# Two expert stages: each half of the tokens sorted once, slots ordered by levels of tiles, waits by level

## The chip, the core and the metric

The kernel runs on one core of one Trainium2 chip. The metric is device time in microseconds, from the first to the last instruction of one launch; smaller is better. All data is fp32 or the 32-bit type that TensorE reads as fp32r.

## The reference

An image batch (8, 128, 32, 32) goes through convolutional attention and whitening, is turned into 8192 tokens of 128 channels (64 tiles of 128 tokens), and passes two attention layers, each followed by a mixture of experts with 8 experts of which every token uses two:

```
probs = softmax(logits); top_p, top_idx = top_k(probs, 2)      # layer 2: gelu, hidden 512
t = t + sum_k w_k * (gelu(LN(t) @ W1[e_k] + b1[e_k]) @ W2[e_k] + b2[e_k])
h = silu(x @ w1[e].T) * (x @ w3[e].T); y = h @ w2[e].T         # layer 3: silu, hidden 341
t = t + sum_k gate_k * y[e_k]
```

Between the two lies window attention over 32 tokens. What is computed is the same before and after the change.

## The kernel before

**Sorting.** Each expert stage routes its tokens in two parts of 32 tiles (`PT`). `Route.place_in_pieces` works on VectorE (DVE): it finds the two best experts, counts tokens by expert, and works out `places`, the row to which each token's copy goes. Rows are slots of 256 rows (`UNIT`), and a slot belongs to one expert, whose number stands in `owners`. A list of `Plan` groups says which tiles are sorted together: `GELU_PLAN` sorts 12, 20 and 32 tiles, `SILU_PLAN` 32, 20 and 12. A group of n tiles takes (2·n·128 + 8·255)//256 slots, so 19, 27 and 39, in all 85 in each stage.

**Sending.** `send_tiles` runs on GpSimd (POOL): two indirect DMAs per tile (one for each chosen expert) write normalised rows into the DRAM scratch `sorted_rows`, with three in flight (`FLIGHT`).

**Units.** `Units` runs the slots as a software pipeline of NU + 4 steps on TensorE (PE). In step s it multiplies slot s-2 up, transposes slot s and multiplies slot s-4 down; its end frees the steps of ScalarE (ACT) and DVE of the same number. SyncE (SP) loads the slot's rows four ahead (`load(u)` waits for the end of step u-4) and stores results (`store(u)`); both stand in one queue. A load that is the first of its group also waits until all DMAs of the group's tiles have landed. In each step DVE drains the down product, makes the low half of x, copies the expert's weights, in silu gates the hidden values, adds results of earlier tiles that are due (`adds`, start step and group) and then runs one piece of the placing of part 1. That placing begins at step 0, and its sends follow on POOL.

**Fetching.** `Units.bring` on POOL waits until a group's slots are stored, and then issues two indirect DMAs per tile that read `sorted_results` into `fetch` buffers of 4 tiles (8 DMAs). There are two such buffers, so the fetch of one waits until the tiles fetched two buffers earlier are added. `add_result` adds two rows per token on DVE.

**Order of the work.** Queues are in program order, and a `Block` ends when all engines are through. The gelu stage has a routing block (part 0 placed; 16 sends; PE then computes biases behind `placed`), and a block with the units and the first half's window attention, which adds the remaining tiles four per step and in which POOL, behind its last fetch, makes the low halves of the silu weights (L2420). The silu stage has a block with the second window attention and the routing (part 0 is placed in its first step), then the silu units; at their end the last tiles are fetched and added and the tokens stored to `out`.

## Time and profile before

| what | value |
|---|---|
| median of 3 runs | 1424.36 us (1424.33 to 1430.51) |
| the profiled execution: time, span | 1423.12 us, 1421.4 us |
| PE busy | 1188.9 us, 84% |
| DVE busy | 919.4 us, 65% |
| POOL busy (issue of indirect DMAs above all) | 582.9 us, 41% |
| ACT busy | 560.4 us, 39% |
| indirect DMAs: sends, fetches | 256, 256 |

Some 1.7 us lie around the span. The clock that TensorE is granted is 1.00 of full through most of the gelu and silu units and 0.50 in the routing. In a timeline row "x9" means that nine instructions were merged; the row's second number is then the time from the first's start to the last's end. An idle time stands in brackets with what ended it.

### The profile page before, as it was taken

The page shows a single profiled execution, that of the slowest core. Times are in us where ns is not written, and L with a number is a line of the kernel's source. Part 1 is how long each engine was busy: PE and PEld are TensorE (multiplying, and loading weights), DVE is VectorE, ACT ScalarE, POOL GpSimd, SP SyncE. Part 2 cuts the span into 40 slices and gives each one's busy share as a digit, 9 for nine tenths or more (in the row PEclk, how much of TensorE's full clock was granted, in tenths as well). Part 3 has the DMA queues.
Part 4 walks back from the last instruction along what each step waited for, and adds up shares of the span by engine and source line. Part 5 has one row for each costly group of instructions (what it writes and reads, how often), then busy time and mean ns, then how long its engine had stood idle before and what let it go on. Part 6 is the DMA issues. An engine that isn't in the chain of part 4 may idle for free. (4 is left out here: it accounts for less than half of the span.)

```text
span 1421.4 us, 31172 instructions
## 1 busy us (share of the span) xinstructions
PE 1188.9 (84%) x11614; PEld 1028.8 (72%) x11614; DVE 919.4 (65%) x2231; ACT 560.4 (39%) x1293; POOL 582.9 (41%) x639
## 2 busy tenths in 40 slices
PE   7999998888574999999996673858589999999960
PEld 4555556668564999999994453636489999999960
DVE  4777775579671754466652876575539777788862
ACT  3444442245461655555554531543323333232310
POOL 3000002000136777774504772067300774566675
PEclk9999999899655999999997885779569999999985
DMA  8300000000502333343424210011012333333343
GB/s 311 129 0 1 0 1 9 1 0 1 142 14 69 115 130 123 123 124 103 115 65 165 53 46 2 1 45 54 28 37 66 116 120 99 103 111 115 108 131 107
DMA packets 85495, 109.63 MB, mean 77 GB/s; under 512 B 18179, under 2 KB 70950, under 8 KB 85094
## 3 DMA queue, kind: packets, MB, share of 16 engines
q1 hardware_dynamic: 65990, 62.92, 14.2%
q0 software_dynamic: 19360, 44.73, 9.9%
q8 instruction: 97, 1.59, 0.5%
q14 instruction: 48, 0.39, 0.1%
HBM read 53.19 MB, written 54.39 MB: 76 GB/s over the span
## 5 line engine op out<-in xcount | busy, mean ns | idle before, releaser
L1425 POOL DMA_INDIRECT sorted_rows<-s_normed,s_places x128 | 135.1, 1055 | 174.9 <-DVE s_places L1366 135.0
L1502 POOL DMA_INDIRECT gx_fetch<-sorted_results,g_places x128 | 131.9, 1030 | 121.8 <-DMA sorted_results<-gx_yq 53.4
L1502 POOL DMA_INDIRECT sx_fetch<-sorted_results,s_places x128 | 136.0, 1062 | 85.5 <-issue 33.1
L1585 PE MATMUL g_bank<-weights,gx_hT 128*128 x1360 | 165.8, 275 | 0.2 <-ACT gx_hT L1613 0.2
L1425 POOL DMA_INDIRECT sorted_rows<-g_normed,g_places x128 | 132.4, 1035 | 64.8 <-issue 35.4
L1585 PEld LDWEIGHTS g_bank<-weights,gx_hT 128*128 128x128 f32 x1360 | 158.5, 192 | 0.6 <-issue 0.6
L1548 PE MATMUL s_bank<-sx_xT_high,sx_w_now 128*128 128x256 f32 (+1 forms) x510 | 151.7, 298 | 1.2 <-DVE sx_hT L1660 0.6
L1550 PE MATMUL s_bank<-sx_xT_high,sx_w_now 128*128 128x256 f32 (+1 forms) x510 | 144.2, 283 | 0.0
L1549 PE MATMUL s_bank<-sx_xT_low,sx_w_now 128*128 128x256 f32 (+1 forms) x510 | 144.0, 282 | 0.0
L1613 ACT ACTIVATE gx_hT<-g_bank,gx_b_now 128x256 f32<-128x256 f32 x340 | 132.8, 481 | 3.1 <-PE g_bank L1585 3.0
L1585 PE MATMUL s_bank<-weights,sx_hT 128*128 (+1 forms) x1020 | 129.7, 276 | 2.9 <-DVE sx_yq L1671 1.4
L1585 PEld LDWEIGHTS s_bank<-weights,sx_hT 128*128 128x128 f32 (+1 forms) x1020 | 120.4, 191 | 6.4 <-issue 6.2
L1606 ACT ACTIVATE sx_xT_high<-s_bank 128x256 fp32r<-128x256 f32 x85 | 32.7, 385 | 225.5 <-PE s_bank L1585 210.1
L237 PE MATMUL attended<-probs,vs 128*128 128x512 f32 x256 | 120.3, 593 | 0.0
L339 ACT ACTIVATE probs<-score,nmax 128x1024 f32<-128x1024 f32 x64 | 71.3, 1115 | 113.1 <-DVE nmax L281 113.1
L281 DVE TENSOR_REDUCE nmax<-score 128x1 f32<-128x1024 f32 x64 | 78.2, 1223 | 45.6 <-PE score L226 45.6
L1548 PE MATMUL g_bank<-gx_xT_high,gx_w_now 128*128 128x256 f32 x340 | 104.0, 306 | 3.1 <-DVE gx_w_now L1643 2.0
L1669 DVE TENSOR_TENSOR gx_yq<-g_bank,weights 128x256 f32<-128x256 f32 x85 | 36.1, 425 | 99.8 <-PE g_bank L1585 97.5
L1550 PE MATMUL g_bank<-gx_xT_high,gx_w_now 128*128 128x256 f32 x340 | 96.9, 285 | 0.0
L1549 PE MATMUL g_bank<-gx_xT_low,gx_w_now 128*128 128x256 f32 x340 | 96.9, 285 | 0.0
L1606 ACT ACTIVATE gx_xT_high<-g_bank 128x256 fp32r<-128x256 f32 x85 | 32.7, 385 | 155.1 <-PE g_bank L1585 127.6
L1548 PEld LDWEIGHTS s_bank<-sx_xT_high,sx_w_now 128*128 128x128 f32 (+1 forms) x510 | 91.3, 179 | 1.7 <-issue 1.7
(423 smaller groups left out, 2718.2 us busy)
## 6 DMA issues: line engine op xcount, KB each, us to landing
gx_xq<-sorted_rows SPq DMA_DIRECT2D x85, 128.0 KB, 2.1
sorted_results<-gx_yq SPq DMA_DIRECT2D x85, 128.0 KB, 2.0
sx_xq<-sorted_rows SPq DMA_DIRECT2D x85, 128.0 KB, 2.1
sorted_results<-sx_yq SPq DMA_DIRECT2D x85, 128.0 KB, 2.0
sorted_rows<-zeros POOLq DMA_DIRECT2D x19, 512.0 KB, 11.2
feats<-in_x SPq DMA_DIRECT2D x8, 512.0 KB, 8.0
out<-tokens SPq DMA_DIRECT2D x16, 256.0 KB, 3.9
s_raw<-in_silu_up SPq DMA_DIRECT2D x1, 2736.0 KB, 10.0
```

The lines of the kernel that those rows point to most:

```text
L237: done = pe.matmul(out[:, HALF * h:HALF * h + HALF], vs[s % 4][:, :], probs[s % 4][:, HALF * h:HALF * h + HALF], start=(n == 0), stop=(n = ...
L281: dve.tensor_reduce(nmax[s % 4][:, :], score[s % 2][:, :], AX.X, ALU.max, negate=True).then_inc(max_ready, 1)
L339: act.activation(probs[s % 4][:, :], score[s % 2][:, :], ACT.Exp, bias=nmax[s % 4][:, 0:1], accum_out=zsum[s % 4][:, 0:1]).then_inc(exp_do ...
L1425: pool.indirect_dma_start(out=sorted_rows[g], out_offset=bass.IndirectOffsetOnAxis(ap=places[:, at, r:r + 1], axis=0), in_=normed[:, at, : ...
L1502: pool.indirect_dma_start(out=fetch[n % 2][:, i, r, :], out_offset=None, in_=self.sorted_results[g], in_offset=bass.IndirectOffsetOnAxis(a ...
L1548: pe.matmul(out, left[:, part, columns], right[0][:, :], start=True, stop=False)
L1549: pe.matmul(out, left[:, part, columns], right[1][:, :], start=False, stop=False)
L1550: pe.matmul(out, left[:, part + 1, columns], right[0][:, :], start=False, stop=True)
L1585: done = pe.matmul(down[u % 2][:, P * k:P * k + C], hT[u % 2][0:width, i, P * k:P * k + P], self.w_down[0:width, bass.ds(e, 1), i, :].rear ...
L1606: act.activation(xT[u % 2][0][:, :], self.turned[u % 2][:, 0:UNIT], ACT.Copy).then_inc(self.x_high, 1)
L1613: done = act.activation(hT[i][:, k, :], up[i][k // 2][:, k % 2, :], ACT.Gelu, bias=self.b_now[u % 4][:, k:k + 1])
L1669: dve.tensor_tensor(self.yq[u % 4][:, :, :], product, bias, ALU.add).then_inc(self.y_ready, 1)
```

## The change

Each part is one group: both plans have two groups of 32 tiles, 39 slots each, 78 in all. Within a group the slots are ordered by levels. A level is a number of tiles n with a kind: FULL levels end, for each expert, at the last slot that the first n tiles fill whole; BEGUN levels end at the last slot that they have begun. A load then waits for the tiles of its level (`tiles_needed`), and the fetch of the first n tiles waits for the slots up to a BEGUN level (`ready_tiles`). By the plan's arithmetic, gelu loads wait for 12 tiles at slot 0, 16 at slot 5, 24 at slot 9, 32 at slot 17, 48 at slot 39, all 64 at slot 48; silu loads for 32 at slot 0, 44 at slot 39 and 64 at slot 44. The gelu fetches wait for 39 slots (tiles to 32), 62 (to 48), 70 (to 56) and 78; the silu fetches for 23 (to 16), 39 (to 32), 58 (to 44), 66 (to 52), 74 (to 60) and 78. The placing has more instructions, since it shifts rows by level and finds owners by level. The silu fetches get four buffers, which lie in the `normed` tiles of part 0. The gelu adds begin at step 50 (before: 46 and 60), the silu adds at steps 45 and 73 (before: 49 and 77). Of scratch filled with zeros there are 94 slots of 128 KB in place of 85.

```diff
-GELU_PLAN = Plan([12, 20, 32], [(0, 2), (2, 3)])
-SILU_PLAN = Plan([32, 20, 12], [(0, 1), (1, 3)])
+FULL, BEGUN = False, True
+GELU_PLAN = Plan([[(12, FULL), (16, FULL), (24, FULL), (PT, BEGUN)],
+                  [(16, FULL), (16, BEGUN), (24, BEGUN), (PT, BEGUN)]])
+SILU_PLAN = Plan([[(16, BEGUN), (PT, BEGUN)],
+                  [(12, FULL), (12, BEGUN), (20, BEGUN), (28, BEGUN), (PT, BEGUN)]])
...
+    def units_of(self, tiles):
+        return (2 * tiles * P + E * (UNIT - 1)) // UNIT
+    def full_units_of(self, tiles):
+        return max(0, -(-(2 * tiles * P - E * (UNIT - 1)) // UNIT))
+    def tiles_needed(self, u):
+        g = self.group_of[u]
+        for n, begun in self.levels[g]:
+            if not begun and u - self.first_unit[g] < self.full_units_of(n):
+                return self.first_tile[g] + n
+        return self.first_tile[g + 1]
...
@@ place_in_pieces
-        for i, g in enumerate(groups):
-            steps.did(dve.tensor_tensor(of_group(before, i), of_group(before, i),
-                                        shift[:, i, :].unsqueeze(1).to_broadcast([P, plan.tiles[g], E]), ALU.add))
+        steps.did(dve.tensor_tensor(by_expert(count), by_expert(before), at_level(change, 0), ALU.add))
+        for i in range(1, L):
+            steps.then(dve.tensor_tensor(by_expert(passing), by_expert(before), at_level(from_row, i - 1), ALU.is_ge))
+            steps.then(dve.tensor_tensor(by_expert(passing), by_expert(passing), at_level(change, i), ALU.mult))
+            steps.then(dve.tensor_tensor(count[:, :], count[:, :], passing[:, :], ALU.add))
+            if i % 2 == 0:
+                yield
...
@@ Units.bring
+            for first, end, units in plan.ready_tiles(g):
+                for i in range(4):
+                    pool.wait_ge(self.y_stored[i], 16 * len(range(i, units, 4)))
+                for n in range(first // SEND, end // SEND):
+                    if n >= len(fetch):
+                        pool.wait_ge(self.added_both, (n + 1 - len(fetch)) * SEND)
...
@@ Units.sync, load(u)
-            if u == plan.first_unit[g]:
-                self.sent.wait_landed(sp, 2 * plan.first_tile[g + 1])
+            if u == 0 or plan.tiles_needed(u) > plan.tiles_needed(u - 1):
+                self.sent.wait_landed(sp, 2 * plan.tiles_needed(u))
...
-                          owners, group_rows, group_results, "gx_", banks, ((46, 0), (60, 1)), Tools(nc, brief))
+                          owners, group_rows, group_results, "gx_", banks, ((50, 0),), fetch, Tools(nc, brief))
...
-                      group_rows, group_results, "sx_", banks, ((49, 0), (77, 1)))
+                      group_rows, group_results, "sx_", banks, ((45, 0), (73, 1)), fetch)
```

Three places in the order of the engines follow. The first is DVE in the gelu routing block, where part 0 is placed: `g_room` holds all work arrays, the last rows end the slot numbers from which `g_places` is cut. (Semaphores are shown under the name that first used their number.) Before:

```order
L1343 TENSOR_TENSOR g_room<-g_room 128x12x8 [waits vs_ready]
L1343 TENSOR_TENSOR g_room<-g_room 128x20x8
L1351 TENSOR_TENSOR g_room<-g_room 128x96 [waits gr_exp_done,vs_ready]
L1351 TENSOR_TENSOR g_room<-g_room 128x160
L1354 TENSOR_REDUCE gr_slot_no<-g_room 128x32 [waits vs_ready]
L1351 TENSOR_TENSOR g_room<-g_room 128x96 [waits vs_ready]
L1351 TENSOR_TENSOR g_room<-g_room 128x160
L1354 TENSOR_REDUCE gr_slot_no<-g_room 128x32 [waits vs_ready]
```

The same place of the change:

```order
L1389 TENSOR_TENSOR g_room<-g_room,gr_change 128x256 [waits vs_ready]
L1391 TENSOR_TENSOR g_room<-g_room,gr_from_row 128x256
L1392 TENSOR_TENSOR g_room<-g_room,gr_change 128x256 [waits vs_ready]
L1393 TENSOR_TENSOR g_room<-g_room 128x256 [waits vs_ready]
L1391 TENSOR_TENSOR g_room<-g_room,gr_from_row 128x256 [waits vs_ready]
L1392 TENSOR_TENSOR g_room<-g_room,gr_change 128x256 [waits vs_ready]
L1393 TENSOR_TENSOR g_room<-g_room 128x256 [waits vs_ready]
L1391 TENSOR_TENSOR g_room<-g_room,gr_from_row 128x256 [waits vs_ready]
L1392 TENSOR_TENSOR g_room<-g_room,gr_change 128x256 [waits vs_ready]
L1393 TENSOR_TENSOR g_room<-g_room 128x256 [waits vs_ready]
L1400 TENSOR_TENSOR g_room<-g_room 128x256 [waits gr_exp_done,vs_ready]
L1401 TENSOR_REDUCE gr_slot_no<-g_room 128x32 [waits vs_ready]
```

One add by group has become one add and three chained instructions for each further level; each waits for the one ahead of it.

The second is SP at the start of the gelu units: rows with four semaphores wait for sent tiles, the row "x3" is loads of slots 6 to 8, the last row is the load of slot 10. Of the change:

```order
L1576 DMA gx_xq<-sorted_rows_0 128x256 [waits qk_high,gx_stepped,proj_ready,x_loaded7]
L1576 DMA gx_xq<-sorted_rows_0 128x256 [waits gx_stepped] x3
L1582 DMA sorted_results_0<-gx_yq 128x256 [waits gx_y_ready]
L1576 DMA gx_xq<-sorted_rows_0 128x256 [waits qk_high,gx_stepped,proj_ready,x_loaded7]
L1582 DMA sorted_results_0<-gx_yq 128x256 [waits gx_y_ready]
L1576 DMA gx_xq<-sorted_rows_0 128x256 [waits gx_stepped]
```

The loads of slots 5 and 9 now wait for sent tiles, and stores stand behind the load of slot 9; before, the first such row behind slot 0 was slot 19.

The third is POOL in the silu fetches, at the first wait for added tiles. Before, in the third set of eight:

```order
L1502 DMA sx_fetch<-sorted_results_0,s_places 128x128 [waits sx_fetched0]
L1502 DMA sx_fetch<-sorted_results_0,s_places 128x128 [waits sx_fetched1,sx_added_both]
L1502 DMA sx_fetch<-sorted_results_0,s_places 128x128 [waits sx_fetched2]
L1502 DMA sx_fetch<-sorted_results_0,s_places 128x128 [waits sx_fetched0]
L1502 DMA sx_fetch<-sorted_results_0,s_places 128x128 [waits sx_fetched1]
```

The change, in the fifth set:

```order
L1554 DMA s_normed<-sorted_results_0,s_places 128x128 [waits sx_fetched1]
L1554 DMA s_normed<-sorted_results_0,s_places 128x128 [waits sx_fetched2]
L1554 DMA s_normed<-sorted_results_0,s_places 128x128 [waits sx_fetched0]
L1554 DMA s_normed<-sorted_results_0,s_places 128x128 [waits sx_fetched1]
L1554 DMA s_normed<-sorted_results_0,s_places 128x128 [waits sx_y_stored3,sx_added_both,sx_y_stored2,sx_fetched2,sx_y_stored1,sx_y_stored0]
```

The fetches run four sets ahead of the adds in place of two, and the wait for stores stands inside a group.

## Rows read from the trace of the kernel before

**Rows 1.** Windows by stage: busy us (x instructions) by engine, PEclk, DMA share, GB/s
```profile
36.00:72.00 36.00, 36.00 (x124) 21.38 (x123) 25.57 (x46) 15.57 (x26) 0.00 (x0) 1.00 0.30 122
441.00:756.00 315.00, 296.61 (x2552) 295.02 (x2552) 170.77 (x460) 161.12 (x430) 184.33 (x176) 0.97 0.35 109
1045.00:1377.00 332.00, 322.44 (x2722) 317.28 (x2722) 266.39 (x581) 101.67 (x260) 183.19 (x165) 0.98 0.34 101
```
**Rows 2.** Timeline of SP, gelu units: slots 0 to 8, slot 9, slot 84
```profile
451.88 16.12 SPq L1524 DMA_DIRECT2D gx_xq<-sorted_rows  x9
...
471.13 0.32 SPq L1524 DMA_DIRECT2D gx_xq<-sorted_rows  x1
...
729.89 0.32 SPq L1524 DMA_DIRECT2D gx_xq<-sorted_rows  x1
```
**Rows 3.** Timeline of SP, silu units: slot 18, slot 84
```profile
1103.15 0.32 SPq L1524 DMA_DIRECT2D sx_xq<-sorted_rows  x1
...
1348.88 0.32 SPq L1524 DMA_DIRECT2D sx_xq<-sorted_rows  x1
```
**Rows 4.** Timeline of PE: biases in the gelu routing; transposes of slot 9
```profile
414.96 0.63 PE L1759 MATMUL gr_bank<-ident,g_bias 32*128 32x32 f32 x2 [1.39 <-DVE g_places L1366]
...
483.31 0.38 PE L1573 MATMUL g_bank<-ident,gx_xq 128*128 128x128 f32 x2
```
**Rows 5.** Timeline of DVE, routing of silu part 0: two chained instructions
```profile
914.24 0.42 DVE L1292 TENSOR_TENSOR sr_mask<-sr_logits,sr_best 128x256 f32<-128x256 f32 x1
914.70 0.43 DVE L1295 TENSOR_TENSOR sr_mask<-sr_mask,sr_rank 128x256 f32<-128x256 f32 x1
```
**Rows 6.** Timeline of POOL, gelu sends: number 24 and number 48
```profile
449.58 0.96 POOL L1425 DMA_INDIRECT sorted_rows<-g_normed,g_places  x1 [0.31 <-issue]
...
482.01 0.96 POOL L1425 DMA_INDIRECT sorted_rows<-g_normed,g_places  x1 [0.30 <-issue]
```
**Rows 7.** Waits, 745 to 880 us: total us, times, longest
```profile
DVE tokens L1710 <- DMA gx_fetch<-sorted_results,g_places: 5.9, 4, 2.7
```
**Rows 8.** Timelines of POOL and DVE, end of the first window attention
```profile
847.37 12.09 POOL L2420 TENSOR_TENSOR weights<-s_raw,weights 128x684 fp32r<-128x684 f32 x8
...
849.26 10.73 DVE L1710 SCALAR_TENSOR_TENSOR tokens<-gx_fetch,g_gates,tokens 128x128 f32<-128x128 f32 x8 [1.93 <-DMA gx_fetch<-sorted_results,g_places]
```
**Rows 9.** Timeline of DVE, silu: step 10 begins, its placing piece, step 11 begins
```profile
1087.28 0.42 DVE L1671 COPY sx_yq<-s_bank 128x256 f32<-128x256 f32 x1
...
1089.90 0.66 DVE L1343 TENSOR_TENSOR sr_before<-sr_before,sr_shift 128x160 f32<-128x160 f32 x2
...
1092.24 0.42 DVE L1671 COPY sx_yq<-s_bank 128x256 f32<-128x256 f32 x1
```
**Rows 10.** Timeline of POOL: silu sends 1, 64; fetches 1, 33, 40, 118, 128
```profile
1100.10 1.40 POOL L1425 DMA_INDIRECT sorted_rows<-s_normed,s_places  x1 [88.95 <-DVE s_places L1366]
...
1191.97 0.96 POOL L1425 DMA_INDIRECT sorted_rows<-s_normed,s_places  x1 [0.30 <-issue]
1210.03 0.98 POOL L1502 DMA_INDIRECT sx_fetch<-sorted_results,s_places  x1 [17.10 <-DMA sorted_results<-sx_yq]
...
1267.00 0.94 POOL L1502 DMA_INDIRECT sx_fetch<-sorted_results,s_places  x1 [4.09 <-DVE tokens L1710]
...
1276.94 0.94 POOL L1502 DMA_INDIRECT sx_fetch<-sorted_results,s_places  x1 [0.30 <-DMA sx_fetch<-sorted_results,s_places]
...
1401.00 0.95 POOL L1502 DMA_INDIRECT sx_fetch<-sorted_results,s_places  x1 [0.30 <-issue]
...
1413.48 0.94 POOL L1502 DMA_INDIRECT sx_fetch<-sorted_results,s_places  x1 [0.30 <-issue]
```
**Rows 11.** Instructions on the silu places, the fetches: min/median/max ns, first and last start
```profile
L1502 POOL DMA_INDIRECT sx_fetch<-sorted_results,s_places x128: 938/945/1609, 1210.0 to 1413.5; - x128
```
**Rows 12.** Timeline of DVE: last down product of the silu units
```profile
1375.42 0.42 DVE L1671 COPY sx_yq<-s_bank 128x256 f32<-128x256 f32 x1 [0.60 <-PE s_bank L1585]
```
**Rows 13.** Time from issue to landing: slot loads, us min/median/max
```profile
DMA to landing us min/median/max: 1.9/2.1/2.8
```

More of the change, by code:

```diff
@@ L184, in _ @@
             fills = 0
[L185 removed]
+            for rows in blank:
                 for at in range(0, rows.shape[0], 8 * P):
@@ L1327, in place_in_pieces @@
[L1327 to L1332 removed]
+        steps.then(dve.tensor_reduce(until[:, L - 1, :], by_expert(count), AX.X, ALU.add))
@@ new lines, in place_in_pieces @@
+        steps.then(dve.tensor_tensor_scan(running, self.ones_row[:, 0:E], until[:, L - 1, :], 0.0, ALU.mult, ALU.add))
+        steps.then(dve.tensor_tensor(begin, running, until[:, L - 1, :], ALU.subtract))
+        yield
+        for i, (n, _) in enumerate(levels[:-1]):
+            steps.did(dve.tensor_tensor(until[:, i, :], by_expert(before)[:, :, n - 1], begin, ALU.subtract))
+        steps.settle()
+        steps.did(dve.tensor_tensor(before[:, :], before[:, :], count[:, :], ALU.subtract))
@@ new lines, in place_in_pieces @@
+        whole = [begun for _, begun in levels].index(BEGUN)
+        for at, more in ((slice(0, whole), -1), (slice(whole, L), 1)):
+            if at.start < at.stop:
+                steps.did(dve.tensor_scalar(flat(until[:, at, :]), flat(until[:, at, :]), more * (UNIT - 1) / 2.0,
+                                            1.0 / UNIT, ALU.add, ALU.mult))
+        steps.settle()
+        steps.then(dve.tensor_scalar(flat(until), flat(until), ROUND, None, ALU.add))
+        steps.then(dve.tensor_scalar(flat(until), flat(until), -ROUND, float(UNIT), ALU.add, ALU.mult))
@@ new lines, in place_in_pieces @@
+        yield
+        steps.did(dve.tensor_tensor(before[:, :], before[:, :], self.held.get(part, self.ahead[part])[:, 0:E * PT], ALU.add))
+        steps.did(dve.tensor_copy(cells[:, 0, :], until[:, 0, :]))
+        steps.did(dve.tensor_tensor(flat(cells[:, 1:, :]), flat(until[:, 1:, :]), flat(until[:, 0:L - 1, :]),
+                                    ALU.subtract))
+        steps.did(dve.tensor_tensor(from_row[:, 0:L - 1, :], until[:, 0:L - 1, :],
+                                    begin.unsqueeze(1).to_broadcast([P, L - 1, E]), ALU.add))
@@ L1339, in place_in_pieces @@
-        steps.did(dve.tensor_tensor(flat(shift), flat(shift), flat(total), ALU.subtract))
-        steps.then(dve.tensor_tensor(before[:, :], before[:, :], self.held.get(part, self.ahead[part])[:, 0:E * PT], ALU.add))
-        yield
-        for i, g in enumerate(groups):
-            steps.did(dve.tensor_tensor(of_group(before, i), of_group(before, i),
-                                        shift[:, i, :].unsqueeze(1).to_broadcast([P, plan.tiles[g], E]), ALU.add))
-        steps.settle()
+        steps.then(dve.tensor_tensor(flat(shift[:, 1:, :]), flat(shift[:, 1:, :]), flat(until[:, 0:L - 1, :]),
+                                     ALU.subtract))
@@ L1349, in place_in_pieces @@
         for r in range(2):
-            for i, tiles in enumerate(tiles_of):
-                steps.did(dve.tensor_tensor(work[:, tiles, :], masks[r][:, tiles, :], of_group(before, i),
-                                            ALU.mult))
-            steps.settle()
+            steps.then(dve.tensor_tensor(work[:, :, :], masks[r][:, :, :], by_tile(count), ALU.mult))
             steps.then(dve.tensor_reduce(self.slot_no[:, :, r], work[:, :, :], AX.X, ALU.add))
@@ L1454, in __init__ @@
         chunks = len(kind.chunks)
-        self.fetch = [t.sbuf(f"{tag}fetch{i}", [P, SEND, 2, C]) for i in range(2)]
+        self.fetch = fetch
         self.xq = [brief.sbuf(f"{tag}xq{i}", [P, KT, C]) for i in range(4)]
```

148 lines of the change are left out of this document (78 added, 70 removed).

## The prediction

> **What bounds the kernel now.** I read the windows by stage first. In the gelu units PE is busy 296.6 of 315 us and in the silu units 322.4 of 332 [rows 1], at a granted clock of 0.97 and 0.98: both run at the pace of PE's steps. The load of a slot is freed by the end of a step, so SP's timeline gives the pace: from slot 9 to slot 84 of gelu 258.8 us for 75 steps, 3.45 us a step [rows 2]; in silu from slot 18 to 84 245.7 us for 66, 3.72 us [rows 3]. Then I read POOL. In silu it waits 89 us for the places of part 1, issues 64 sends, waits 17.1 us for stores, and from then on fetches in turns with the adds [rows 10]. DVE drains the last down product at 1375.4 [rows 12]; the span ends 46 us later, at the pace of POOL: 1.25 us from one fetch to the next (ten spacings from 1401.00 to 1413.48), and 7.9 us behind the last fetch for its landing, eight adds and a store to `out` (1421.4 - 1413.48) [rows 10]. So the silu stage ends with a tail of POOL's, and the steps ahead of it are PE's.
>
> **Gelu stage.** *Seven slots fewer* take 7 x 3.45 = 24.2 us off PE's steps; all their work (PE, DVE, ACT, a load and a store) goes with them.
>
> *Placing part 0.* A chained instruction on 256 elements costs 0.46 us from start to start [rows 5]. Four levels need 3 x 3 such, 4.1 us. Some five small instructions more at about 0.2 us (half such a spacing, my estimate) add 1.0, and the adds and products that were written in two pieces give about 0.2 back: +5 us (bounds 3 and 7). PE starts the biases only when DVE has made the places: it waited 1.39 us for them at 414.96 [rows 4], and its chain of biases and scores then runs to the end of the block. So all 5 us lie on the path. The sends shift with it, and so does everything behind. The owners, three levels more, come behind the places and are covered by PE's biases; without that cover they would cost 3 us.
>
> *Loads by level.* Send 24 was issued at 449.58 and the first load left at 451.88 [rows 2, 6], so a send has landed 2.3 us after its issue; a load lands 2.1 us later [rows 13]. Slot 9 now waits for 24 tiles, that is for send 48, issued at 482.01 [rows 6]: its rows are there at 482.0 + 2.3 + 2.1 = 486.4, and PE transposed slot 9 at 483.3 [rows 4]. Both shift by the same 5 us, so PE waits 3.1 us where it waited for nothing; I take +3 (bounds 1 and 5, as a send's landing varies). On SP the store of slot 1 and the loads behind stand behind this load; they need half a microsecond each and are in time. For slot 17 all 64 sends of part 0 have 8 steps (27 us) more for 16 sends (22 us at the pace of rows 6, 32.4/24 = 1.35), so with the wait just taken it is not late; slots 39 and 48 have over 20 us of room.
>
> *Placing part 1 in the steps.* A step of gelu leaves DVE 1.5 us or so (170.8 busy of 315 us, with the added tiles) [rows 1]. The piece with two levels is 6 x 0.46 = 2.8 us and 0.9 of other work, so it overruns by 2, the next by 0.5; the step buffers of PE take part of it: +2 (bounds 0 and 4). Places come a piece later; the sends of part 0 end only about then.
>
> *Fetches.* POOL is through with the 32 tiles of part 0 late, by the adds (every 3.5 steps four tiles), and two sets of part 1 are in the buffers before the units end. The stage: -24.2 + 5 + 3 + 2 = **-14**.
>
> **First window attention.** DVE waited 5.9 us in four places for fetches [rows 7]; two sets now stand ready. The other six sets, 48 fetches, follow the adds, so the last comes only some 3 us earlier. Behind it POOL makes the low weights for 12.09 us, and the eight adds of DVE that fall into them take 10.73 us [rows 8]. That block stays and moves earlier with the fetches: **-3.5** (bounds 0 and -6). The Trainium skill, page "SBUF — State Buffer", section "SBUF: two separate sides", says that a DVE instruction with two SBUF inputs and a GpSimd one that reads SBUF lock each other out for a whole instruction; by that rule, the trace agrees: eight adds needed 10.73 us while POOL's block ran.
>
> **Second window attention.** DVE places part 0 in its first step and PE waits for what comes behind: two levels for one, so three chained instructions (1.4), some small ones (0.9) and a second round of owners (1.2): **+3.5** (bounds 2 and 6).
>
> **Silu stage.** *Placing part 1.* Here a step leaves DVE no buffer: step 10 took 2.62 us for its fixed work and 2.34 for its piece, 4.96 in all, beside 3.7 of a plain step [rows 9]. With five levels the pieces are: piece 10 3.6 us (+1.3 against now), piece 11 2.7 (+1.6), piece 12 1.5 (+0.4), pieces 7 to 9 together +0.8, so +4.1 up to the places; behind them the owners of five levels, +1.0 for the first two and 0.2 each, and the gates: together about +6 for the stage. The places come two steps (7.4 us) and these 4.1 us later: the first send goes from 1100.1 to 1111.8, counted from the same start of the stage.
>
> *Steps.* The last down product is at 1375.4 - 7 x 3.72 + 6 = 1355.4.
>
> *POOL.* The sends took 91.9 us for 63 spacings, 1.458 each [rows 10]: the last is at 1203.7, the first fetch at 1205. Slot 44 needs send 64 landed and loaded, 1208; PE comes to it at about 1218. The first adds (step 45, about 1224) find their set landed at 1218. Four buffers let POOL run without waiting for adds: a set of eight takes 11.4 us at 1.42 (7 spacings from 1267.00 to 1276.94) [rows 10], the adds take four tiles every 3.5 steps, 13.0 us, so POOL gains on them by 1.6 us a set and starts four sets ahead. The waits for slots 58, 66, 74 are past before POOL comes to them (slot 74 is stored at about 1345, its set is due at 1358). So POOL issues its 128 fetches in one run: at 1.43 until 1355 that is 105, the other 23 at 1.25 to 1.29 take 28 us. The last is at 1383.5, and the span ends 7.9 later at 1391.4. Against 1421.4: **-30** (bounds -22 and -45).
>
> **Zeros.** 94 slots for 85, 1.2 MB more, behind the image loads; PE is busy 36.0 of 36 us in the window in which they end and DMA share is 0.30 [rows 1]. Nothing there waits for DMA: 0. Without that cover it would be 1.2 MB at the 122 GB/s of the row, 10 us.
>
> **Sum.** -14 - 3.5 + 3.5 - 30 = -44 on the profiled 1423.1 us: 1379. The median of the runs is 1.2 us above the profiled time, so **1380 us**.
>
> **The rivals.**
> *A. The forecast* (chance 0.58): POOL sets the silu end, PE the rest; 1374 to 1387.
> *B. The steps set the end.* If POOL kept up, only the last set would lie behind the last store: 1355.4 + 2 + 8 x 1.25 + 7.9 = 1375, 16 us less: 1364. For it speaks that the level waits are arranged so; against it that 192 DMAs at 1.43 from 1112 need 275 us and the steps left are 244. Chance 0.08.
> *C. POOL runs slower than in the rows.* DVE now adds while POOL has no pauses, and the spacing could be 0.1 us more over the 169 issues beside the steps: +17, 1397. The longest fetch was 1.609 us, the median 0.945 [rows 11]. Chance 0.15.
> *D. DVE's pieces and the sends cost twice* what I take (5 + 3 + 2 + 3.5 + 6, partly): +11, 1391. Chance 0.13.
> *E. POOL's issue blocked by DVE: slower than before.* If each of the 169 issues beside the steps took the longest one's 1.609 plus the gap of 0.30, in place of 1.43, the chain would be 81 us longer and the kernel 1460. It decides against the change from a mean spacing of 1.69 us on (44/169 more). In the rows the spacing stays at 1.42 to 1.46 with and without adds, so 0.03. The Trainium skill, "SBUF — State Buffer", section "A bandwidth-pool intuition that's wrong (but worth ruling out)", gives this the other way: a DMA whose descriptors GpSimd writes takes about 3100 ns beside a DVE copy in place of 620. By its figure the sum would be 169 x 1.7, some 280 us, worse; the trace does not bear that out, its longest issue beside the steps is 1.609 us.
> *F. The gain is eaten elsewhere*, so that the time stays (0.03): it would need the stage starts to wait for something that the trace of before doesn't show.
>
> **How the numbers follow.** The time is A's. The range takes in B's side down to 1368 (the window bounds and no stall at slot 9) and C and D up to 1395; outside are half of B, the long end of C, E and F, about 0.15. 0.5%, 7 us, is about what a measurement of this kernel tells from no change. A to D are all faster by more: 0.94; F 0.03; E 0.03.
>
> **What the changed profile would show.** Slot loads 75 steps apart in gelu still at 3.45 us, with one wait of PE of about 3 us for the load of slot 9; the gelu biases some 5 us later; in silu the first send of part 1 some 12 us later than before, counted from the stage's first load, no pause of POOL for added tiles over a microsecond, about 20 fetches behind the last down product and 36 us from there to the end. The prediction is wrong if POOL pauses between sends and fetches, if PE waits for slot 44 or at step 45 for DVE, or if the clock row of a units stage falls below 0.95.

## The result and the profile after

| | us | ratio to before |
|---|---|---|
| before | 1424.34 (1423.21 to 1430.51) | |
| changed | 1382.84 (1379.73 to 1387.72, 4 runs) | 0.9706, 95% interval 0.9674 to 0.9737 |
| the same kernel, measured again | 1386.27 (1380.55 to 1390.75, 6 runs) | 0.9725, 0.969 to 0.9759 |

The forecast was 1380 us. The profiled run took 1379.73 us with a span of 1377.7; the span is 43.7 us shorter than before's 1421.4.

The windows by stage of the changed kernel (busy us and instructions of PE, PEld, DVE, ACT, POOL; granted clock, DMA share, GB/s):
```profile
36.00:72.00 36.00, 36.00 (x117) 20.67 (x117) 26.16 (x48) 15.98 (x27) 0.00 (x0) 1.00 0.35 143
444.00:743.00 299.00, 274.52 (x2342) 272.15 (x2342) 169.32 (x464) 148.30 (x395) 199.04 (x192) 0.96 0.37 112
1030.00:1362.00 332.00, 298.78 (x2498) 292.72 (x2498) 261.22 (x587) 93.73 (x239) 204.11 (x185) 0.95 0.36 110
```
Against [rows 1], the units stages have shrunk and PE's share in them has fallen a little. In gelu PE is busy 274.5 of 299 us (296.6 of 315 before). The silu window is as long as before and now reaches 21 us behind the last down product: from the first load to that product PE is busy 298.8 of 310.4 us (322.4 of 330.0 before), at a granted clock of 0.98 as before, and POOL 190 in place of 182. The zeros' window is as full as before, so the larger scratch costs nothing there.

**Gelu.** PE's row for the biases, and SP's slots 0 to 8, 9 and 77:
```profile
417.97 0.63 PE L1811 MATMUL gr_bank<-ident,g_bias 32*128 32x32 f32 x2 [6.34 <-DVE g_places L1413]
```
```profile
454.89 16.39 SPq L1576 DMA_DIRECT2D gx_xq<-sorted_rows  x9
...
487.17 0.32 SPq L1576 DMA_DIRECT2D gx_xq<-sorted_rows  x1
...
716.11 0.32 SPq L1576 DMA_DIRECT2D gx_xq<-sorted_rows  x1
```
PE waits 6.34 us for the places, where it waited 1.39 [rows 4]: 4.95 us more. (The work ahead of it came 1.9 us earlier than in the profile of before, which nothing in the change explains; so the row itself stands only 3.0 us later.) The first load moves with it, from 451.88 to 454.89 [rows 2]. Slot 9's load went out at 471.13 and now goes out at 487.17, held by send 48; slot 77's, the last, goes out at 716.11, 13.8 us before slot 84's of the kernel before. The waits of PE from 440 to 760 us (total, times, longest):
```profile
PE g_bank L1625 <- DMA gx_xq<-sorted_rows: 18.2, 2, 15.6
```
15.6 us is the wait for slot 0, which stood there before; the other, 2.6 us, is new and is slot 9's. It costs more than itself. Windows ahead of it, in it and behind it, and PE's rows:
```profile
483.00:486.40 3.40, 3.40 (x32) 3.40 (x31) 2.86 (x8) 3.35 (x7) 2.49 (x4) 1.00 0.14 47
486.40:489.30 2.90, 0.34 (x4) 0.14 (x3) 2.71 (x12) 2.29 (x5) 2.29 (x3) 1.00 0.44 144
489.30:494.10 4.80, 3.93 (x20) 3.70 (x21) 0.27 (x1) 0.00 (x0) 3.16 (x4) 0.68 0.73 222
```
```profile
489.29 0.44 PE L1625 MATMUL g_bank<-ident,gx_xq 128*128 128x128 f32 x2 [2.56 <-DMA gx_xq<-sorted_rows]
490.59 3.48 PE L1637 MATMUL g_bank<-weights,gx_hT 128*128 x16 [0.87 <-issue]
...
495.78 1.95 PE L1637 MATMUL g_bank<-weights,gx_hT 128*128 x16
```
PE stood idle from 486.7 to 489.3; in the 4.8 us behind that the granted clock was 0.68 on average, so for most of it at the lower level, 1.2 GHz, and the 16 matmuls of a down product took 3.48 us, 1.95 one step later. DVE's drains of the down product (L1721) show the sum of both and, behind it, the steps that place part 1:
```profile
486.44 0.42 DVE L1721 TENSOR_TENSOR gx_yq<-g_bank,weights 128x256 f32<-128x256 f32 x1 [0.16 <-DVE g_room L1354]
...
494.29 0.42 DVE L1721 TENSOR_TENSOR gx_yq<-g_bank,weights 128x256 f32<-128x256 f32 x1 [4.72 <-PE g_bank L1637]
...
498.30 0.42 DVE L1721 TENSOR_TENSOR gx_yq<-g_bank,weights 128x256 f32<-128x256 f32 x1 [1.13 <-PE g_bank L1637]
...
503.57 0.42 DVE L1721 TENSOR_TENSOR gx_yq<-g_bank,weights 128x256 f32<-128x256 f32 x1 [0.16 <-DVE g_room L1393]
...
507.72 0.42 DVE L1721 TENSOR_TENSOR gx_yq<-g_bank,weights 128x256 f32<-128x256 f32 x1 [0.16 <-DVE gr_slot_no L1401]
510.49 0.42 DVE L1721 TENSOR_TENSOR gx_yq<-g_bank,weights 128x256 f32<-128x256 f32 x1 [0.16 <-DVE gr_slot_no L1401]
```
The two steps up to 494.29 took 4.00 and 7.85 us; in the trace of before the same two took 3.43 and 3.05. That is 5.4 us, 2.6 of them the wait.

The other profiles tell how much of the rest is the clock. Nine of them, this one among them, have the same gelu code. In three PE waited only 1.8 us for slot 9, and the clock did not fall behind the wait. One of these is the kernel without early fetches below; the same stretch of it, from the end of the wait on, and its PE rows:
```profile
488.67:493.47 4.80, 3.98 (x33) 3.75 (x34) 1.86 (x9) 1.68 (x6) 3.23 (x4) 1.00 0.76 235
```
```profile
488.67 0.44 PE L1625 MATMUL g_bank<-ident,gx_xq 128*128 128x128 f32 x2 [1.79 <-DMA gx_xq<-sorted_rows]
489.93 2.05 PE L1637 MATMUL g_bank<-weights,gx_hT 128*128 x16 [0.82 <-issue]
```
Its down product took 2.05 us in place of 3.48. In these three, the two steps and the one behind them together cost 2.8 to 3.1 us more than before, 1.0 to 1.3 beyond the wait. In the six others PE waited 2.5 to 3.1 us, the clock fell in each, and the three steps cost 5.1 to 6.0, 2.6 to 3.0 beyond the wait. So of the 5.4 us here 2.6 are the wait, some 1.2 come with it even at full clock, and some 1.6 are the clock's.

Then the piece with two levels makes a step of 5.27 us and the next one of 4.15, released by DVE itself, but the two behind them take 2.77 and 2.79: PE had worked ahead. The eight steps from 494.29 on took 29.4 us, before 27.8: the pieces cost 1.5.

**The two attentions.** The block behind the last fetch has moved from 847.37 to 830.63 [rows 8]; POOL's part lasts 12.09 us as before, DVE's eight adds 10.33 in place of 10.73:
```profile
830.63 12.09 POOL L2471 TENSOR_TENSOR weights<-s_raw,weights 128x684 fp32r<-128x684 f32 x8
...
832.92 10.33 DVE L1762 SCALAR_TENSOR_TENSOR tokens<-gx_fetch,g_gates,tokens 128x128 f32<-128x128 f32 x8 [3.17 <-DMA gx_fetch<-sorted_results,g_places]
```
From gelu's last down product to the end of these adds it is 103.0 us, 106.0 before: 3.0 less. From there to silu's first load it is 187.2 us, 185.4 before: 1.8 more. The placing of part 0 that stands in the second stretch costs more than that: from its first level to the owners DVE took 5.88 us before (923.74 to 929.62) and takes 9.35 (907.06 to 916.41), 3.5 more, and 9.33 to 9.35 in every later profile. The work behind it, which the change leaves as it is, took 115.8 us before, 114.0 here and 113.4 to 120.4 in the later profiles, so the 1.8 is no price of the edit.

**Silu.** The stage's first load is at 1030.42 (1045.40 before):
```profile
1030.42 4.24 SPq L1576 DMA_DIRECT2D sx_xq<-sorted_rows  x5
```
POOL's first and last send of part 1, first and last fetch:
```profile
1097.00 1.43 POOL L1476 DMA_INDIRECT sorted_rows<-s_normed,s_places  x1 [100.26 <-DVE s_places L1413]
...
1189.04 0.95 POOL L1476 DMA_INDIRECT sorted_rows<-s_normed,s_places  x1 [0.31 <-issue]
1190.30 0.98 POOL L1554 DMA_INDIRECT s_normed<-sorted_results,s_places  x1 [0.30 <-issue]
...
1369.75 0.94 POOL L1554 DMA_INDIRECT s_normed<-sorted_results,s_places  x1 [0.30 <-issue]
```
The 17.10 us of idle time before the first fetch and the 4.09 before fetch 33 [rows 10] are gone. POOL goes from sends to fetches without a pause, 92.0/63 = 1.461 us a send and 179.4/127 = 1.413 us a fetch. DVE's end of the stage:
```profile
1340.79 0.42 DVE L1723 COPY sx_yq<-s_bank 128x256 f32<-128x256 f32 x1 [0.60 <-PE s_bank L1637]
1341.13 6.58 DVE L1762 SCALAR_TENSOR_TENSOR tokens<-s_normed,s_gates,tokens 128x128 f32<-128x128 f32 x20
1351.22 2.73 DVE L1762 SCALAR_TENSOR_TENSOR tokens<-s_normed,s_gates,tokens 128x128 f32<-128x128 f32 x8 [3.51 <-DMA s_normed<-sorted_results,s_places]
1362.37 2.75 DVE L1762 SCALAR_TENSOR_TENSOR tokens<-s_normed,s_gates,tokens 128x128 f32<-128x128 f32 x8 [8.42 <-DMA s_normed<-sorted_results,s_places]
1372.29 2.69 DVE L1762 SCALAR_TENSOR_TENSOR tokens<-s_normed,s_gates,tokens 128x128 f32<-128x128 f32 x8 [7.16 <-DMA s_normed<-sorted_results,s_places]
```
Behind the last down product (1340.79) the end takes 36.9 us, 46.0 before [rows 12]; 21 of the fetches start in it, 28 before. DVE waits there three times for a fetched set: the tail is still POOL's.

**How far a median carries.** Two profiles of the changed kernel itself differ by 7.1 us. From gelu's last down product to silu's first load, a stretch that no experiment edits, the first took 290.2 us and the second 295.3. The last part of that stretch, of the first profile and then of the second (columns as above):
```profile
940.25:1030.42 90.17, 65.30 (x1645) 52.89 (x1645) 46.57 (x115) 30.33 (x62) 42.53 (x44) 0.72 0.10 35
```
```profile
942.39:1037.71 95.32, 70.25 (x1622) 56.66 (x1621) 45.75 (x114) 30.52 (x62) 41.82 (x43) 0.67 0.09 33
```
All 5.1 us lie in it: the same matmuls took PE 5 us more at a granted clock of 0.67 in place of 0.72, PE being idle a quarter of both. So differences of a few us are read below as positions inside one trace, counted from the stage's first load. These spread too, but less: in the five profiles with the changed kernel's silu code (its own two and the three kernels edited in gelu alone) the end of the stage lies at 346.9 to 348.7. In the nine with its gelu code, the last gelu load comes 258.5 to 261.4 us after the first: 258.5 to 258.8 in the three whose clock did not fall at slot 9, 260.6 to 261.4 in the six others.

### The profile page after: what moved, and what is told of

Read it like the earlier page. It is cut to its first block and busy times, and to the rows that moved or that the text cites. A ratio compares the mean times of both kernels' runs of the same rounds, so it can differ in the third digit from the quotient of the medians.

```text
span 1377.7 us, 30030 instructions
## 1 busy us (share of the span) xinstructions
PE 1138.8 (83%) x11180; PEld 977.8 (71%) x11180; DVE 916.7 (67%) x2252; ACT 539.9 (39%) x1237; POOL 582.8 (42%) x641
## 5 line engine op out<-in xcount | busy, mean ns | idle before, releaser
L1476 POOL DMA_INDIRECT sorted_rows<-g_normed,g_places x128 | 130.8, 1022 | 74.4 <-issue 35.7
L1554 POOL DMA_INDIRECT s_normed<-sorted_results,s_places x128 | 138.1, 1079 | 42.6 <-issue 37.3
L1637 PE MATMUL g_bank<-weights,gx_hT 128*128 x1248 | 153.6, 277 | 1.0 <-issue 0.9
L1637 PEld LDWEIGHTS g_bank<-weights,gx_hT 128*128 128x128 f32 x1248 | 146.7, 193 | 1.6 <-issue 1.6
L1600 PE MATMUL s_bank<-sx_xT_high,sx_w_now 128*128 128x256 f32 (+1 forms) x468 | 139.2, 297 | 1.8 <-DVE sx_hT L1712 1.2
L1602 PE MATMUL s_bank<-sx_xT_high,sx_w_now 128*128 128x256 f32 (+1 forms) x468 | 132.5, 283 | 0.0
L1601 PE MATMUL s_bank<-sx_xT_low,sx_w_now 128*128 128x256 f32 (+1 forms) x468 | 132.2, 283 | 0.0
L1637 PE MATMUL s_bank<-weights,sx_hT 128*128 x936 | 120.7, 279 | 3.8 <-issue 2.2
L1665 ACT ACTIVATE gx_hT<-g_bank,gx_b_now 128x256 f32<-128x256 f32 x312 | 121.9, 481 | 3.1 <-PE g_bank L1637 3.0
L1637 PEld LDWEIGHTS s_bank<-weights,sx_hT 128*128 128x128 f32 x936 | 111.7, 193 | 8.1 <-issue 8.0
L1600 PE MATMUL g_bank<-gx_xT_high,gx_w_now 128*128 128x256 f32 x312 | 95.5, 306 | 4.9 <-DVE gx_w_now L1695 2.0
L1721 DVE TENSOR_TENSOR gx_yq<-g_bank,weights 128x256 f32<-128x256 f32 x78 | 33.2, 425 | 89.2 <-PE g_bank L1637 87.6
L1601 PE MATMUL g_bank<-gx_xT_low,gx_w_now 128*128 128x256 f32 x312 | 88.9, 285 | 0.0
L1602 PE MATMUL g_bank<-gx_xT_high,gx_w_now 128*128 128x256 f32 x312 | 88.7, 284 | 0.0
```

Of the source, the lines that this page charges most:

```text
L1476: pool.indirect_dma_start(out=sorted_rows[g], out_offset=bass.IndirectOffsetOnAxis(ap=places[:, at, r:r + 1], axis=0), in_=normed[:, at, : ...
L1554: pool.indirect_dma_start(out=fetch[n % len(fetch)][:, i, r, :], out_offset=None, in_=self.sorted_results[g], in_offset=bass.IndirectOffse ...
L1600: pe.matmul(out, left[:, part, columns], right[0][:, :], start=True, stop=False)
L1601: pe.matmul(out, left[:, part, columns], right[1][:, :], start=False, stop=False)
L1602: pe.matmul(out, left[:, part + 1, columns], right[0][:, :], start=False, stop=True)
L1637: done = pe.matmul(down[u % 2][:, P * k:P * k + C], hT[u % 2][0:width, i, P * k:P * k + P], self.w_down[0:width, bass.ds(e, 1), i, :].rear ...
```

## The experiments

Positions in the silu stage, us from its first load:

| kernel | first send of part 1 | first fetch | last down product | last fetch | end |
|---|---|---|---|---|---|
| changed | 66.6 | 159.9 | 310.4 | 339.3 | 347.3 |
| changed, again | 66.3 | 159.4 | 310.1 | 339.1 | 347.1 |
| two buffers | 66.6 | 159.8 | 310.2 | 356.3 | 364.2 |
| no early fetch | 58.6 | 151.3 | 309.8 | 394.3 | 402.2 |
| memsets ahead of the sends | 73.4 | 164.5 | 317.4 | 344.9 | 352.7 |
| sends wait for step 18 | 75.1 | 169.4 | 312.2 | 349.0 | 356.9 |
| places 3 steps earlier | 56.2 | 148.4 | 311.2 | 337.2 | 345.2 |
| two pieces in every step | 45.6 | 138.0 | 317.8 | 343.8 | 351.8 |
| places and adds earlier | 56.2 | 149.4 | 312.0 | 336.0 | 344.0 |
| places, adds and finer gelu pieces | 55.4 | 148.6 | 312.5 | 334.7 | 342.7 |

**Two fetch buffers for silu.**
```
-fetch = [... for i in range(0, PT, 2 * SEND)]
+fetch = [... for i in range(0, PT // 2, 2 * SEND)]
```


> The changed kernel with two fetch buffers in silu in place of four. Theory (GpSimd sets the silu end, and four buffers let it run without waiting for adds): GpSimd pauses for added tiles in most sets, the sets 12 to 15 lie about or behind the last step, and the time from the last down product to the end grows from 37 to some 45 us: 8 us slower than the change, about 1388 in a profiled execution. Rival (the adds by step set the pace anyway, buffers are spare): within 2 us of the change.

Measured 1397.76 us (ratio 0.9795, 0.9758 to 0.9832). Nothing moves up to the first fetch, and then the end comes 16.9 us later. POOL's waits from 1170 us on (total, times, longest):
```profile
POOL s_normed L1554 <- DVE tokens L1762: 20.6, 7, 4.7
```
The changed kernel has no such row. The buffers are worth 17 us of the stage, twice what I expected. With two, POOL is held at the adds' pace from fetch 17 (186.5 us after the first load, 182.7 in the changed kernel) to fetch 89 (303.8 and 284.7): 13.0 us a set of eight in place of 11.3. At the last down product 34 fetches are still to start, in place of 21.

**No fetch of silu part 1 before all slots are stored.**
```
-[(12, FULL), (12, BEGUN), (20, BEGUN), (28, BEGUN), (PT, BEGUN)]
+[(12, FULL), (PT, BEGUN)]
-((45, 0), (73, 1))
+((45, 0),)
```
The second pair puts the adds of part 1 behind the steps.

> The changed kernel with two levels in silu part 1 (12 tiles for the loads, all 32 for the fetches), so that no tile of part 1 is fetched before the last slot is stored; the adds of part 1 all stand behind the steps. Theory: 64 fetches at 1.26 us, 81 us, follow the last store, so the tail grows from 37 to about 90 us; the three levels fewer give 4 back: about 50 us slower than the change, 1430, so that the slots saved alone would not make the kernel faster. Rival (the levels of the fetches give little, since GpSimd is the bound from the sends on): under 20 us slower.

Measured 1439.67 us (1.0096, 1.0064 to 1.0128): 1% above before, so nothing of the gain is left. Places come 8.0 us earlier with two levels in place of five, the last down product stays, and the end comes 55.0 us later (50 expected). POOL's timeline has it in one row:
```profile
1343.09 0.94 POOL L1554 DMA_INDIRECT s_normed<-sorted_results,s_places  x1 [70.00 <-DMA sorted_results<-sx_yq]
```
So sorting a half once is of use in silu only with the levels by which part 1 is fetched early: with 64 fetches behind the last store the stage takes 402.2 us, more than the 376.0 of before with its seven slots more.

**One level for the gelu slots of part 0.**
```
-[(12, FULL), (16, FULL), (24, FULL), (PT, BEGUN)]
+[(12, FULL), (PT, BEGUN)]
```


> The changed kernel with gelu part 0 in two levels, 12 tiles and all 32, so that slots from 5 on wait for all 64 sends of part 0. Theory: TensorE stands about 39 us at slot 5 for send 64, the wait at slot 9 (2.6 us) goes, two levels of placing fewer give 2.8 us on the path: about 33 to 37 us slower than the change, 1415. Rival (the loads' levels are spare, as later steps have room for the sends): under 10 us slower.

Measured 1412.84 us (0.9898, 0.9852 to 0.9945). SP, and PE's waits from 440 to 760 us:
```profile
451.94 52.94 SPq L1576 DMA_DIRECT2D gx_xq<-sorted_rows  x9
```
```profile
PE g_bank L1625 <- DMA gx_xq<-sorted_rows: 51.5, 2, 35.7
```
The loads wait for all 64 sends, and PE waits 33.3 us more (51.5 - 18.2). The two levels less gave 3.0 us back ahead of the first load (PE waited 3.29 us for the places in place of 6.34), so a level costs 1.5 us there, three chained instructions. Together 30 us, which is what the medians differ by; the expected 33 to 37 took the wait as 39 us, and it was 35.7.

**GpSimd's chain of the silu stage begins later.** Two kernels. The first puts eight memsets of 128x1024 between the places and the first send, into a tile that nothing reads:

> The changed kernel with 8 memsets of 128x1024 on GpSimd (some 8 us) between the places of silu part 1 and its first send. Theory (GpSimd's chain of sends and fetches sets the end): the end moves by the whole 8 us, TensorE's last down product stays within 2 us. Rival (TensorE's steps and the last store set the end, with 16 us of room on GpSimd): no change.

Measured 1390.52 us (0.975, 0.9714 to 0.9787): the end is 5.5 us later in the trace, but so are PE's steps, by 7.0. The rows of POOL, DVE and PE at the memsets say why:
```profile
1100.60 7.21 POOL L2576 MEMSET s_idle<- 128x1024 f32 x8 [104.14 <-DVE s_places L1413]
```
```profile
1101.26 7.28 DVE L1695 CAST sx_w_now<-weights 128x1368 fp32r x1
```
```profile
1109.60 0.55 PE L1600 MATMUL s_bank<-sx_xT_high,sx_w_now 128*128 128x256 f32 x1 [5.75 <-DVE sx_hT L1712]
```
A CAST of 0.87 us lasted 7.28 us, until the eighth memset was through. The kernel delayed both chains and does not tell them apart. So another one holds the sends back by a wait alone:
```
 pool.wait_ge(route.placed, 2)
+pool.wait_ge(units.stepped, 18)
```


> GpSimd's sends of the silu stage's second half are held back without any work on GpSimd: they wait for the start of TensorE's 18th step, which in the changed kernel lies 74.4 us after the stage's first load, where the first send is issued at 66.6. So GpSimd's chain begins 7.8 us later, and nothing else is touched. In the kernel with memsets in this place the end came 5.5 us later, but the memsets also held a CAST of VectorE for 7.28 us and with it the steps of TensorE (last down product 7.0 us later), so that run does not tell which of the two chains set the end. Here the last down product should stay at 310.4 us after the first load. If GpSimd's chain sets the end, the last fetch goes from 339.3 to about 346.5 us after the first load and the end from 347.3 to 354.5: 1390 us. If the steps set it, both stay and the time with them: 1383 us.

Measured 1392.6 us (0.9769, 0.9739 to 0.9799). Its first send and last fetch on POOL, and the last down product on DVE:
```profile
1108.95 1.42 POOL L1476 DMA_INDIRECT sorted_rows<-s_normed,s_places  x1 [110.61 <-PE s_bank L1637]
...
1382.86 0.94 POOL L1554 DMA_INDIRECT s_normed<-sorted_results,s_places  x1 [0.30 <-issue]
```
```profile
1346.13 0.42 DVE L1723 COPY sx_yq<-s_bank 128x256 f32<-128x256 f32 x1 [0.58 <-PE s_bank L1637]
```
First send 8.5 us later, last fetch 9.7, end 9.6 (some 7 to 8 expected of each), last down product only 1.9 (nothing expected). So POOL's chain sets the end of the changed kernel.

**The gelu sends with a later pause.** `SENT_EARLY` from 8 to 12 tiles.

> The changed kernel with 12 tiles sent in the gelu routing block in place of 8, so that GpSimd's 4.1 us pause at the end of that block no longer stands between send 16 and send 17. Theory (the first load of gelu waits for send 24): the first load leaves 4 us earlier against the places of part 0, and the kernel is 4 us faster than the change. Rival (the block now ends later, with the last of its 24 sends, and costs the same): no change.

Measured 1383.76 us (0.9706, 0.9674 to 0.9738): nothing. POOL's first send of this kernel, and the one behind the change of block:
```profile
421.52 1.12 POOL L1476 DMA_INDIRECT sorted_rows<-g_normed,g_places  x1 [25.26 <-DVE g_places L1413]
...
455.70 0.96 POOL L1476 DMA_INDIRECT sorted_rows<-g_normed,g_places  x1 [3.19 <-POOLq L2308]
```
The pause has moved from 443.74, where it was 4.06 us, to 455.70. The first load comes 33.6 us after the first send in place of 36.1, but slot 9's comes 67.5 us after it in place of 68.4: it waits for 24 tiles, and the pause lies ahead of the 48th send in either case. What PE gains at slot 0 it waits at slot 9: 4.3 us there, 2.6 and 3.1 in the two profiles of the changed kernel. The rival's forecast holds, though not for its reason.

**Silu places three steps earlier.** The counts are taken at step 4 and two pieces run in each of steps 0 to 2:
```
+if not kind.gelu: self.COUNT = 4
-next(placing, None)
+for _ in range(2 if not kind.gelu and s < 3 else 1): next(placing, None)
```


> The changed kernel with two placing pieces in each of silu steps 0 to 2 and the counting in step 4 in place of 7, so that the places of part 1 come in step 11 in place of 14. Theory (GpSimd sets the end): first send of part 1 some 8 us earlier, the last down product up to 3 us later, the kernel 8 us faster than the change. Rival (the steps set the end): 0 to 3 us slower.

Measured 1380.4 us (0.9681, 0.9647 to 0.9714), in the trace 2.1 us. The first fetch is 11.5 us earlier, the last and the end 2.1 (the end at 345.2, just outside the spread of 346.9 to 348.7). POOL's waits from 1170 us on:
```profile
POOL s_normed L1556 <- DVE tokens L1766: 6.6, 5, 3.2
...
POOL s_normed L1556 <- DMA sorted_results<-sx_yq: 4.3, 3, 3.2
```
The expectation failed here: adds stand at fixed steps (45 and 73) and stores follow the steps, so a POOL that comes earlier waits for both.

**Two pieces in every step but step 3.** As above with `s != 3`.

> The changed kernel with two placing pieces in every silu step but step 3, and the counting in step 4: the places of part 1 come in step 7. Theory: first send of part 1 some 20 us earlier, the steps 7 us longer in all; GpSimd's chain then ends within a few us of the last set that the last store frees, so that the kernel is about 10 us faster than the change and not 20. Rival (the steps set the end already): 7 us slower.

Measured 1389.64 us (0.9747, 0.9713 to 0.9781). The first send is 21 us earlier and is of no use; the steps are 7.4 us longer, POOL waits 18.3 us for adds and 6.8 for stores, and the end is 4.6 us later. This is the rival of the expectation: 6.8 us slower in the medians, 7 expected by it.

**Finer pieces of the gelu placing.** A yield behind each level's work in part 1.

> The changed kernel with a placing piece of its own for each level (shifts and owners) in gelu part 1. Theory (the two-level piece overruns the room of a step): the gelu steps lose 2 to 3 us less, the kernel is 2.5 us faster than the change; the sends of part 1 begin 7 us later and are still in time for slot 48. Rival (DVE's total work counts, not its spread): no change.

Measured 1380.63 us (0.968, 0.9647 to 0.9714). The eight steps behind the wait at slot 9 took 27.8 us in place of 29.4 (27.5 in the other kernel with these pieces, the last one below), so the finer pieces give back the whole of the 1.5 us, not the 2.5 expected. From the first gelu load to the last it is 259.7 us, in place of 261.4 where PE waited as long for slot 9. In the median this can't be told from nothing.

**The adds moved too, and both stages together.** To "places three steps earlier" adds that begin at steps 41 and 69, and then the finer gelu pieces as well:
```
-((45, 0), (73, 1))
+((41, 0), (69, 1))
```


> The silu stage's second half gets its places 3 steps earlier, and the additions of the results begin 4 steps earlier too (step 41 in place of 45, step 69 in place of 73). In the trace with the places alone 3 steps earlier, GpSimd's first fetch came 11.5 us earlier relative to the stage's first load, but the last one only 2.1 us: between them GpSimd waited 6.6 us for VectorE's additions to give a fetch buffer back and 4.3 us for stores of results, which the changed kernel did not. If it was the additions' fixed steps that ate the gain, the 6.6 us come back: last fetch about 332 us after the stage's first load in place of 337.2, time about 1375 us. The rival: the fetches' own spacing (1.41 us) and the stores set it, the waits for additions only fall elsewhere, and the time stays at 1380 us.

> The same with the finer pieces of placing in the gelu stage (a yield after each level). In the trace of the finer pieces alone, the last gelu slot loaded 259.7 us after the first, against 261.2 us in the changed kernel. If the two gains add, this is 1.5 us under the kernel with the silu edits alone, about 1373.5 us; if the finer pieces bring nothing, both give the same time.

> The changed kernel once more on the chip of the other two, so that they can be set against it: 1380 to 1385 us. The difference of each of the other two to this one is their gain: 6 to 9 us if the additions' steps ate the gain of the earlier places, 1 to 3 us if not.

On the same chip the changed kernel took 1386.27 us, the first of these 1380.88 (0.9688, 0.9655 to 0.9721) and the second 1376.48 (0.9654, 0.9622 to 0.9687), the fastest of all. POOL's waits in the first, and one row of its timeline:
```profile
POOL s_normed L1556 <- DMA sorted_results<-sx_yq: 5.3, 2, 4.2
...
POOL s_normed L1556 <- DVE tokens L1766: 0.6, 2, 0.3
```
```profile
1337.93 0.94 POOL L1556 DMA_INDIRECT s_normed<-sorted_results,s_places  x1 [4.15 <-DMA sorted_results<-sx_yq]
```
The waits for adds fell from 6.6 to 0.6 us, as expected, but the last fetch came only at 336.0, not at 332: POOL now stands 4.15 us for a store, and 24 fetches are still to come. From this row the steps have begun to set the end, and starting POOL earlier still should bring nothing; that was not tried.

Against the changed kernel's profile the silu stage is 3.2 and 4.5 us shorter, of which some 2 came with the places alone. The two have the same silu code, so the 1.3 between them is spread. The medians are 5.4 and 9.8 us lower, but not by silu alone. The first's profile also has a gelu stage 3.0 us shorter, which it does not edit: it is one of the three whose clock did not fall at slot 9. The second has the finer pieces but also that fall, and its last gelu load comes 260.0 us after the first, 1.4 less than in the changed kernel and 1.5 more than in the first. Its stretch between the stages, not edited either, took 292.5 us in place of 295.3. So that the two gains add, as expected, is not shown.

## Why the prediction was right

| term | predicted | measured |
|---|---|---|
| gelu: seven slots, with the three costs below | -14 | -11.8 |
| placing part 0 on the path | +5 | +4.95 |
| PE's wait for slot 9 | +3 | +5.4 |
| pieces of part 1 in the steps | +2 | +1.5 |
| first attention | -3.5 | -3.0 |
| second attention | +3.5 | +1.8 |
| silu, first load to end | -30 | -28.7 |
| ahead of the change | 0 | -1.9 |

The measured column is made of the two profiles: gelu 754.01 to 740.25 at the last down product, less the 1.9 us ahead of it; from there to silu's first load 291.4 and 290.2 us, parted at the end of the adds beside POOL's block; silu 376.0 and 347.3.

- **The pace of the gelu steps** held, 3.44 us before and after: seven slots are 24.1 us, and with the three costs that gives -12.2, against -11.8 measured.
- **Placing part 0** was right in mechanism and size.
- **"PE waits 3.1 us where it waited for nothing; I take +3"** is the term that was mis-sized. The wait itself was 2.6 us (3.1 in the second profile), as worked out, but PE came out of it at a granted clock of 0.68, and the two steps cost 5.4. I had priced the idle time alone. In the three profiles where the clock did not fall the cost was 2.8 to 3.1, near the +3, but by a wait of 1.8 and 1.0 to 1.3 beside it. The bound of 5 stood beside the +3 for another reason, a late landing. With one level for the slots the wait became 36 us, so it is the levels that keep it small.
- **Pieces of part 1:** 1.5 us for 2. "The step buffers of PE take part of it" held.
- **First attention** moved with the fetches, and the block of 12.09 us stayed whole. In the second profile the part is only 1.6 us shorter than before.
- **Second attention:** the term was right in mechanism and size, +3.5 in DVE's placing; that the whole stretch shows +1.8 is spread in the work behind it.
- **Silu.** First send at 66.6 us (66.4 predicted), no pause between sends and fetches, 21 fetches behind the last down product (23), 36.9 us to the end (36), overrun of the steps 6.4 (6). Two small errors partly cancel: the fetches beside the steps came at 1.42 us and not 1.43, so that more of them were through, and the 21 behind came at 1.40 and not 1.25 to 1.29. The 66.4 itself should have been 66.2 (1100.1 + 7.4 + 4.1 is 1111.6). The chain came out, and the kernel with the wait for step 18 shows that the chain is the one that sets the end. That answers rival B: the steps did not matter until POOL was started earlier.
- **Rival C** needed 1.53 us a fetch and 1.56 a send; they took 1.413 and 1.461. **Rival E** needed a mean of 1.69. **Rival D** held for one of its terms only. (The 1.609 us that E calls the longest issue beside the steps is the longest fetch; one send took 1.63.) The silu gain stands on two parts, and the runs price them: without early fetches of part 1 the stage loses 55 us, with two buffers 17. What the seven slots are worth in silu by themselves no run shows.
- **Signs of being wrong.** None came: POOL did not pause between sends and fetches, PE waited neither for slot 44 nor at step 45, and the clock of the units stages is 0.96 and 0.95 in the windows, 0.98 in both from the first load to the last down product.
- **What is luck.** That the profile fell within a microsecond of 1380 is: the second profile of the same kernel took 7.1 us more with the same silu stage. The medians, 1382.84 and 1386.27, are 3 and 6 us above the forecast. The silu term is not luck: 347.3 and 347.1 us in the two profiles, 346.0 forecast.

What stays open is why the work ahead of the change took 1.9 us less in this profile. In the nine profiles of this code the first gelu load stands at 454.89 to 456.85, and this one is the earliest, so it is likely the spread of that stretch.

## What to carry to other kernels

Find the engine whose chain ends last and write it out as start, count and spacing; then ask of each edit which of the three it changes. When a chain is started earlier, look for what releases it further down (here adds at fixed steps, then stores): the first of these takes the gain. And a wait put into a full TensorE pipeline costs more than its idle time: here 5.4 us for one of 2.6, behind which the clock was lower, and 3 us for one of 1.8, behind which it was not.

## What the hardware showed

**An issue that meets a CAST is stretched.** POOL's spacing of 1.46 us beside the silu steps, where a plain issue of 0.95 and the 0.30 behind it make 1.25, comes from single issues. POOL's and DVE's rows of the changed kernel:
```profile
1184.17 1.58 POOL L1476 DMA_INDIRECT sorted_rows<-s_normed,s_places  x1 [0.30 <-issue]
1186.05 0.95 POOL L1476 DMA_INDIRECT sorted_rows<-s_normed,s_places  x1 [0.30 <-issue]
1187.31 1.42 POOL L1476 DMA_INDIRECT sorted_rows<-s_normed,s_places  x1 [0.30 <-issue]
```
```profile
1184.05 0.87 DVE L1695 CAST sx_w_now<-weights 128x1368 fp32r x1 [0.31 <-issue]
1187.74 0.87 DVE L1695 CAST sx_w_now<-weights 128x1368 fp32r x1 [0.31 <-issue]
```
The two long issues, 1.58 and 1.42 us, are those in which a CAST falls; the one between takes 0.95. So it is in all 64 sends of the stage. 37 have no CAST beside them and take 0.95 to 1.01 us, and 3 in which the CAST begins 0.58 us or more behind their start take 0.95 or 0.96. The other 24 take 1.19 to 1.62 us and end 0.12 us (13 of them) or 0.83 us (11) behind the end of the CAST. The 25 CASTs in these 92 us add 11.5 us, 0.18 for each send, and two waits for a landing 0.02: 1.255 + 0.18 + 0.02 is the measured 1.46. This was read from rows and not tried by itself.

The Trainium skill, "SBUF — State Buffer", section "SBUF: two separate sides", says that a DVE copy in a 2-port mode and a GpSimd instruction take one port pair as a lock; the trace agrees. The Trainium skill, same page, section "A bandwidth-pool intuition that's wrong (but worth ruling out)" gives 3100 ns for such a DMA beside a copy, and by that figure the chain would be far longer. But it explains the figure as a wait to the end of DVE's instruction and about 115 ns more, and that the trace bears out, in the 13 issues that end 0.12 us behind a CAST: here the cost is bounded by the length of the copy, 0.87 us.

**Memsets hold a CAST too.** Eight memsets on POOL held one CAST from 0.87 to 7.28 us: it did not get in between two of them. That does not hold for every run of POOL instructions: of the eight adds that began beside POOL's eight TENSOR_TENSOR above, seven took 0.84 to 1.59 us each in place of 0.35, about one to each instruction of POOL's. A filler on POOL is thus no neutral delay, it moved the last down product by 7.0 us; the wait in its place moved it by 1.9.
